# Centring x for the first layer norm with one fp32 product, without the rounded part and the remainder

## The chip, the cores and the metric

The kernel runs on one core of a Trainium2 chip. The metric is the device time of one execution in microseconds (us), the median of several runs. A measurement of this kernel repeats within about 0.1%.

## The reference, cut to what matters

Two Swin transformer blocks run on x of shape (16, 28, 28, 64), and a whitening over all tokens follows. Only the first layer norm of each block bears on the change:

```
def layer_norm(x, g, b):
    mu = jnp.mean(x, axis=-1, keepdims=True)
    var = jnp.var(x, axis=-1, keepdims=True)
    return (x - mu) * jax.lax.rsqrt(var + EPS) * g + b

def swin_block_fn(x, shift, mask, ...):
    y = layer_norm(x, ln1_g, ln1_b)
    ...                       # windows of 7x7 tokens, 8 heads, softmax attention
    x = x + out
    z = layer_norm(x, ln2_g, ln2_b)
    z = jax.nn.gelu(z @ fc1_w + fc1_b, approximate=False)
    return x + (z @ fc2_w + fc2_b)
```

## The kernel before, in words

The work is cut into 16 groups (`HALVES`) a block. A group is 392 tokens (`TOK`, eight windows of 49) of each of two images; the 64 channels of the two images share the 128 partitions, so x of a group is a tile of 128 x 392 in `XW`. Each block has an attention part, whose steps run over the groups, and an MLP part, whose steps run over the same groups. Each engine has its order of work written out by hand, and semaphores tie the engines together.

The norm of a group has these stages. TensorE multiplies x with the matrix `centre` (identity minus 1/64 within one image), which gives x minus its mean in the PSUM bank `bX` and counts up `xc_ready`. ScalarE squares it (`square`), TensorE averages the squares (`f_var`), ScalarE adds epsilon (`variance`, line 477), and VectorE computes the inverse root in eight instructions (lines 777 to 786) and the product with the centred x (line 789). That is `z_done`, which also frees `bX`. In the attention part this runs three groups ahead (`AHEAD = 3`).

There are two ways to form the centred x. `f_xc` multiplies `centre` and x as fp32. It serves the groups 0 to 3 of each block, and the MLP part has its own copy of it. `f_xc_split` serves the groups 4 to 15 of each block, in the steps 1 to 12. For it, ScalarE writes x rounded to the type fp32r into `xh` (`x_high`, line 485), GpSimd writes the remainder x minus `xh`, rounded too, into `xl` (`x_low`, line 402), and TensorE adds two products of fp32r operands in one accumulation, `centre_r` with `xh` and `centre_r` with `xl`.

An attention step of TensorE runs in this order: transposed scores of window group 0, the product of the probabilities with v for group 1 of the step before, v of the next step, scores of the next step for window group 0, **the centred x**, the output projection of the group two steps back (`proj`, four records `att,wph`), scores of the next step for window group 1 (its bias products are `bn,dup_r`; they wait for VectorE's row maxima, line 799), the averaged squares (`sq,conb`), k and q, transposed scores of group 1, and the next product with v. ScalarE rounds x behind the copies of k and q (lines 492 and 501) and ahead of the exponentials of window group 1 (line 518). GpSimd takes the remainder behind the two multiplications of the step, `attn` (line 409). SyncE issues all transfers of the steps; none of them carries `xh` or `xl`.

All matmuls of the steps have line 1008, so they are told apart by their operands: `xh,centre_r` and `xl,centre_r` are the two products of the split form, `XW,conb` is an fp32 product with `centre`, and `sq,conb` is one with the matrix of averages. An fp32 matmul stands in the trace as two records with a weight load each, and an fp32r one as one record.

Of the kernel before, what the change touches and what calls it, by code (L numbers as in the profile page):

```python
# [16 lines left out]
HALVES = 2 * PAIRS  # L17
# [40 lines left out]
def build(nc, x, par, gamma, beta, con, out):  # L58

    ctx = ExitStack()  # L60
    with ctx:
        def sb(name, shape, dt=F32):
            return ctx.enter_context(nc.sbuf_tensor(name, shape, dt))

        def sem(name):
            return ctx.enter_context(nc.semaphore(name))
# [54 lines left out]

        epsc = sb("epsc", [128, 1])

        xh = sb("xh", [128, TOK], F32R)
        xl = sb("xl", [128, TOK], F32R)
        sq = sb("sq", [128, TOK])
        lv = [sb(f"lv{i}", [128, TOK]) for i in range(2)]
        ly = sb("ly", [128, TOK])
# [67 lines left out]
        xc_ready, sq_done, var_ready, var_used, ln_link = (  # L196
            sem("xc_ready"), sem("sq_done"), sem("var_ready"), sem("var_used"), sem("ln_link"))

        xh_done, xl_done = sem("xh_done"), sem("xl_done")
        q_ready, k_ready, v_ready, s_ready, mxt_ready, st_ready, av_ready, proj_ready = (  # L200
            sem("q_ready"), sem("k_ready"), sem("v_ready"), sem("s_ready"), sem("mxt_ready"), sem("st_ready"),
            sem("av_ready"), sem("proj_ready"))
# [28 lines left out]
            return XW[blk][:, bass.ds(g * TOK, TOK)]  # L231

        AHEAD = 3
        NSPLIT = HALVES - AHEAD - 1
        NPREP = 6
        NCON, NPAR = 2, 3
        WSTEP = {n: i + 1 for i, n in enumerate(
# [135 lines left out]
        @block.gpsimd  # L373
        def _(pool):
            for k in range(2):
                for name in ("wq", "wk"):
                    nc.gpsimd.memset(P[k][name][:, :], 0.0)
                for name in ("f1", "f2"):
                    nc.gpsimd.memset(P[k][name][:, :, :], 0.0)
            nc.gpsimd.memset(wcol[:, EXPO:EXPO + 1], -0.5).then_inc(s_zero, 1)  # L380
            for i in range(2):
                nc.gpsimd.memset(vbd[i][:, :, :], 0.0)
            nc.gpsimd.memset(ones1[:, :], 1.0)
            for i in range(2):
                nc.gpsimd.memset(tsb[i][:, :, :, CH:CH + 1], 1.0)
            nc.gpsimd.memset(epsc[:, :], LN_EPS).then_inc(s_zero, 1)
            nc.gpsimd.memset(kexp[:, :, :], 0.0).then_inc(s_zero_x, 1)
            for i in range(2):
                nc.gpsimd.memset(qexp[i][:, :, :], 0.0).then_inc(s_zero_x, 1)
            pool.wait_ge(s_zero, 2)  # L390
            pool.wait_ge(s_zero_x, 3)

            for i in range(2):
                for w in range(2):
                    last = nc.gpsimd.memset(vbd[i][64 * w:64 * w + NTOK, :, 16 * w + HD:16 * w + HD + 1], 1.0)
            last.then_inc(s_zero, 1)

            def x_low(blk, g):

                pool.wait_ge(xh_done, NSPLIT * blk + g)  # L400
                pool.wait_ge(xc_ready, HALVES * blk + g + AHEAD)
                nc.gpsimd.tensor_tensor(xl[:, :], xcols(blk, g + AHEAD), xh[:, :].bitcast(F32), ALU.subtract)\
                    .then_inc(xl_done, 1)

            def attn(g, part):

                pool.wait_ge(rec_in[part], 16 * (g + 1))
                pool.wait_ge(proj_ready, g)
                nc.gpsimd.tensor_tensor(  # L409
                    att[:, 4 * part:4 * part + 4, :], osb[part][:, :].rearrange("p (a n) -> p a n", a=4),  # L410
                    rec[part][:, :].rearrange("p (a n) -> p a n", a=4), ALU.mult).then_inc(att_done, 1)

            def step(base, g):
                if g:
                    attn(base + g - 1, 0)
                    attn(base + g - 1, 1)
                if g + 1 + AHEAD < HALVES:
                    x_low(base // HALVES, g + 1)

            pool.wait_ge(s_con, 16 * NCON)  # L420
            for blk in range(2):
                base = HALVES * blk
                for g in range(HALVES):
                    step(base, g)
                attn(base + HALVES - 1, 0)
                attn(base + HALVES - 1, 1)

                if blk:
                    pool.wait_ge(w_dve, WSTEP["shift"])
                for it in range(0, PAIRS):  # L430
                    if blk == 0:
                        pool.wait_ge(mres_done, (it + 1) * 2)
                    pool_relay(pool, blk, it)

            pool.wait_ge(w_dve, WSTEP["trace"])
            nc.gpsimd.tensor_tensor(wcol[:, RSQ:RSQ + 1], wcol[:, TRACE:TRACE + 1], wcol[:, EXPO:EXPO + 1], ALU.pow)\
                .then_inc(w_pool, 1)
# [3 lines left out]
        def _(act):  # L441
# [34 lines left out]
                    act.wait_ge(z_done, g - 1)  # L476
                nc.scalar.activation(lv[buf][:, :], bB[:, 0:TOK], ACT.Identity, bias=epsc[:, 0:1]).then_inc(var_used, 1)  # L477

            def x_high(blk, g):

                if blk:
                    act.wait_ge(relay_done, (g + AHEAD) // 2 + 1)
                act.wait_ge(xc_ready, HALVES * blk + g + AHEAD)
                act.wait_ge(xl_done, NSPLIT * blk + g - 1)
                nc.scalar.activation(xh[:, :], xcols(blk, g + AHEAD), ACT.Copy).then_inc(xh_done, 1)

            def evac_k(p, g1, early=False):

                act.wait_ge(k_ready, g1 + 1)
# [37 lines left out]
            def step(p, base, g, u, first, ahead, tail=None, pair=0):  # L527

                G = base + g
                f = first and base == 0  # L530
                expo(G, 0, f)
                if first:
                    variance(G + 2, u)
                else:
                    o_copy(G - 1, 1, base == 0 and g == 1)
                if tail:
                    tail[0]()
                if ahead > 0:
                    evac_v(G + 1, 1 - u, f)
                if ahead > 2:  # L540
                    square(G + 3)
                    variance(G + 3, 1 - u)
                if ahead > 1:
                    evac_k(p, G + 2, f)
                    evac_q(p, G + 2, u, (G + 1) // 2 + 1)
                if g + 1 + AHEAD < HALVES:
                    x_high(base // HALVES, g + 1)
                expo(G, 1, f)
                if tail:
                    tail[1]()  # L550
                o_copy(G, 0, f)
# [454 lines left out]
        def _(pe):  # L1006
# [4 lines left out]

                mm(bX[:, 0:TOK], centre[:, :], xcols(blk, g - HALVES * blk)).then_inc(xc_ready, 1)

            def f_xc_split(blk, g):

                pe.wait_ge(xl_done, NSPLIT * blk + g)
                mm(bX[:, 0:TOK], centre_r[:, :], xh[:, :], True, False)
                mm(bX[:, 0:TOK], centre_r[:, :], xl[:, :], False, True).then_inc(xc_ready, 1)

            def f_var(g):  # L1020

                pe.wait_ge(sq_done, g + 1)
# [84 lines left out]
            def step(p, blk, g, u, ahead, tail=None, pair=0):  # L1107

                G = HALVES * blk + g
                first = g == 0  # L1110
                nb = 1 - u
                scores_t(p, blk, u, G, 0, u, pair, None if first else lambda i: (exp_done, 4 * G - 1 + i))
                if first:
                    pe.wait_ge(q_done, G + 2)
                    f_var(G + 2)
                else:
                    pv(G - 1, 1, nb)
                if ahead > 0:
                    pe.wait_ge(k_done, G + 2)
                    f_v(p, nb)  # L1120
                    scores(p, blk, nb, G + 1, 0, lambda i: (exp_done, 4 * G + 1 + i))
                if ahead > 2:
                    pe.wait_ge(z_done, G + 3)
                    if first:
                        if blk:
                            pe.wait_ge(relay_done, AHEAD // 2 + 1)
                        f_xc(blk, G + AHEAD)
                    else:
                        f_xc_split(blk, g)
                if g > 1:  # L1130
                    pe.wait_ge(v_done, 2 * G + 4 if ahead > 0 else 2 * G + 2)
                    proj(p, G - 2)
                if ahead > 0:
                    scores(p, blk, nb, G + 1, 1, lambda i: (max_done, 4 * G + 5 + i))
                if tail:
                    tail[0]()
                if ahead > 2:
                    if first:
                        pe.wait_ge(var_used, G + 3)
                    f_var(G + 3)  # L1140
                if ahead > 1:
                    if g > 1:
                        pe.wait_ge(res_done, G - 1)
                    else:
                        pe.wait_ge(v_done, 2 * G + 4)
                    f_qk(p, G + 2, u, (var_used, G + 4) if ahead > 2 else (rx_done, G + 1))
                scores_t(p, blk, u, G, 1, u, pair,
                         (lambda i: (max_done, 4 * G + 7 + i)) if ahead > 0 else lambda i: (exp_done, 4 * G + 1 + i))
                if tail:
                    tail[1]()  # L1150
                if ahead > 0:
                    if ahead > 1:
                        pe.wait_ge(q_done, G + 3)
                    maxt(G + 1)
                pv(G, 0, u, first and blk == 0)
# [345 lines left out]
```

## Time and profile before

| what | value |
|---|---|
| time, median of 3 runs | 910.91 us (910.0 to 911.21) |
| the profiled execution | 913.9 us, of which the span of the trace is 912.1 us |
| mean granted TensorE clock | 0.941 of full speed |
| busy: TensorE, its weight loads, VectorE, ScalarE, GpSimd | 820.0, 565.1, 588.5, 378.6, 218.2 us |
| attention stretches with the 24 split products | 96 to 290 us and 494 to 697 us of the span |

The profile is one execution. The names PE, PEld, DVE, ACT, POOL and SP stand for TensorE's matmuls, its weight loads, VectorE, ScalarE, GpSimd and SyncE. "Idle before" is idle time of the engine ahead of the instruction, and behind the arrow is what ended it; "issue" is idle time in which the engine waited for nothing that the profile shows. Matmuls are pipelined and overlap, so what one costs the stream is the distance between its start and the start of the next, not its own duration. In a view by windows the columns are the window and its length, then the busy time (and instructions) of PE, PEld, DVE, ACT and POOL, the granted clock as a share of full speed, the busy share of the DMA engines and their GB/s. [...]

### The profile page before, as it was taken

Reading aid. Unit: us, or ns where it says so; the run is one execution under the profiler, and the core shown is the slowest. Engines: PE = TensorE matmul, PEld = TensorE weight load, DVE = VectorE, ACT = ScalarE, POOL = GpSimd, SP = SyncE. Lnnn points to the kernel's source line nnn. Section 1 sums busy time; section 2 is a strip of 40 time slices with the busy share of each in tenths; the row PEclk is TensorE's granted clock in tenths of the full one; section 3 lists DMA queues with packets and bytes.
Section 4 is the critical chain, followed back from the end, with each engine's and each line's share of the span. In section 5 each row is a group of like instructions: output and inputs, shape, how many; then the busy total and the mean of one; then the engine's idle time right before and its main releaser. Section 6 shows DMA issues by size and latency. Waiting matters only on the chain.

```text
span 912.1 us, 35605 instructions
## 1 busy us (share of the span) xinstructions
PE 820.0 (90%) x15686; PEld 565.1 (62%) x15686; DVE 588.5 (65%) x1047; ACT 378.6 (42%) x676; POOL 218.2 (24%) x507
## 2 busy tenths in 40 slices
PE   3777899998999889999859999999999989999968
PEld 2645677676776655555436676776667645555648
DVE  2636887676778448888655666767666378887033
ACT  1513445354443344455423444544444345454400
POOL 4000122122120103435400211212211026565100
PEclk9768999999999889999977999999999989999959
DMA  9100121121111110000001111112112110000004
GB/s 225 19 29 24 46 62 56 44 63 57 51 63 48 59 33 10 1 1 0 19 19 32 59 51 52 60 50 66 50 45 68 34 40 0 1 1 0 2 0 142
DMA packets 47662, 38.34 MB, mean 42 GB/s; under 512 B 28564, under 2 KB 46996, under 8 KB 47508
## 3 DMA queue, kind: packets, MB, share of 16 engines
q1 hardware_dynamic: 46496, 33.96, 12.8%
q8 instruction: 124, 2.03, 0.9%
q10 hardware_dynamic: 1012, 2.10, 0.7%
q14 instruction: 30, 0.25, 0.1%
HBM read 18.37 MB, written 4.01 MB: 25 GB/s over the span
## 4 chain that ended last, share of the span: by engine, by line
PE 44%; DVE 3%; issue 2%; DMA 1%; ACT 0%; SPq 0%; POOL 0%; DVEq 0%; ACTq 0%
PE psum L1008 43%; DVE nmax L799 1%; PE psum L1370 1%; DMA dens<-rpk 1%; DMA rec<-dens 0%; DVE kexp L980 0%; ACT lv L477 0%; DVE kexp L982 0%; DVE lt L779 0%; DVE ly L786 0%; DVE lt L780 0%; DVE lt L785 0%; POOL att L409 0%; DVE ly L777 0%; DVE z L789 0%
## 5 line engine op out<-in xcount | busy, mean ns | idle before, releaser
L409 POOL TENSOR_TENSOR att<-osb,rec 128x392 f32<-128x392 f32 x64 | 72.0, 1125 | 425.0 <-DMA rec<-dens 406.0
L799 DVE TENSOR_REDUCE nmax<-psum 113x16 f32<-113x784 f32 x128 | 118.5, 968 | 71.7 <-PE psum L1008 71.7
L518 ACT ACTIVATE pt<-psum 113x784 f32<-113x784 f32 x128 | 98.6, 822 | 122.2 <-PE psum L1008 122.2
L610 ACT ACTIVATE hid<-psum,vecb 128x392 f32<-128x392 f32 x128 | 75.1, 587 | 96.9 <-PE psum L1008 92.4
L1008 PE MATMUL psum<-bt,dup_r 113*113 113x392 f32 x256 | 102.6, 401 | 2.3 <-DVE nmax L799 2.1
L1008 PE MATMUL psum<-z,f 128*128 128x392 f32 x256 | 97.5, 504 | 0.1
L1008 PE MATMUL psum<-hid,f 128*128 128x392 f32 x256 | 89.9, 493 | 0.0
L1008 PE MATMUL psum<-rx,sel_r 128*113 128x392 f32 x256 | 88.6, 346 | 0.0
L1008 PE MATMUL psum<-kexp,qsb 32*49 32x98 f32 x4096 | 73.7, 262 | 10.4 <-issue 9.8
L825 DVE RECIPROCAL rpk<-dpk 64x49 f32<-64x49 f32 x64 | 28.9, 452 | 76.1 <-DMA dpk<-osb 76.0
L1008 PEld LDWEIGHTS psum<-kexp,qsb 32*49 32x49 f32 x4096 | 57.0, 123 | 30.2 <-issue 29.2
L1008 PEld LDWEIGHTS psum<-z,f 128*128 128x128 f32 x256 | 49.3, 194 | 38.5 <-ACT hid L610 3.0
L1008 PEld LDWEIGHTS psum<-hid,f 128*128 128x128 f32 x256 | 48.5, 190 | 35.4
L367 POOL TENSOR_TENSOR XW<-XW,wcol 128x49 f32<-128x49 f32 (+5 forms) x200 | 59.1, 332 | 42.3 <-DVE XW L890 31.2
L1008 PE MATMUL psum<-qexp,ksb 32*49 32x98 f32 x4096 | 68.4, 252 | 0.5 <-issue 0.5
L1008 PE MATMUL psum<-pt,vbd 113*32 113x49 f32 x4096 | 60.8, 210 | 7.0 <-ACT osb L525 5.6
L1008 PEld LDWEIGHTS psum<-qexp,ksb 32*49 32x49 f32 x4096 | 54.3, 118 | 19.0 <-issue 18.6
L1008 PE MATMUL psum<-sq,conb 128*128 128x392 f32 x128 | 61.4, 564 | 5.1 <-ACT sq L592 2.8
L349 POOL COPY XW<-XW 128x64 f32<-128x64 f32 (+2 forms) x192 | 47.5, 304 | 57.0 <-DVE XW L890 57.0
L1008 PEld LDWEIGHTS psum<-pt,vbd 113*32 113x32 f32 x4096 | 51.6, 111 | 14.0 <-issue 8.6
L777 DVE TENSOR_SCALAR ly<-lv 128x392 int32<-128x392 int32 x64 | 23.8, 372 | 56.0 <-ACT lv L477 26.7
L477 ACT ACTIVATE lv<-psum,epsc 128x392 f32<-128x392 f32 x32 | 18.8, 588 | 92.8 <-PE psum L1008 91.5
(154 smaller groups left out, 1321.7 us busy)
## 6 DMA issues: line engine op xcount, KB each, us to landing
rec<-dens SPq DMA_DIRECT2D x64, 196.0 KB
kexp<-ksb SPq DMA_DIRECT2D x128, 49.0 KB
qexp<-qsb SPq DMA_DIRECT2D x128, 49.0 KB
XW<-x_dram SPq DMA_DIRECT2D x14, 196.0 KB, 4.7
out_dram<-XW SPq DMA_DIRECT2D x14, 196.0 KB, 2.4
dpk<-osb SPq DMA_DIRECT2D x64, 12.2 KB
dens<-rpk SPq DMA_DIRECT2D x64, 12.2 KB, 2.6
pt<-w_dram ACTq DMA_DIRECT2D x2, 384.0 KB, 7.4
```

The source lines that it names most:

```text
L349: last = nc.gpsimd.tensor_copy(dst[:, i, jo:jo + jn, ro:ro + rn, co:co + cn], src[:, si, ji:ji + jn, ri:ri + rn, ci:ci + cn])
L367: last = nc.gpsimd.tensor_tensor(dst[:, y0:y0 + rn, q0:q0 + cn], src[:, i, j, r0:r0 + rn, c0:c0 + cn], wcol[:, SHIFTC:SHIFTC + 1].rearrang ...
L409: nc.gpsimd.tensor_tensor(att[:, 4 * part:4 * part + 4, :], osb[part][:, :].rearrange("p (a n) -> p a n", a=4), rec[part][:, :].rearrange( ...
L477: nc.scalar.activation(lv[buf][:, :], bB[:, 0:TOK], ACT.Identity, bias=epsc[:, 0:1]).then_inc(var_used, 1)
L518: nc.scalar.activation(pt[grp][:, b:b + 2, :], SC[0:KROWS, b:b + 2, 0:BANK], ACT.Exp)\
L610: nc.scalar.activation(hid[c], mF1[c % 2][:, 0:TOK], ACT.Gelu, bias=p["vec"][:, FB + c:FB + c + 1]).then_inc(gelu_done, 1)
L777: ln(nc.vector.tensor_scalar(ly[:, :].bitcast(I32), v[:, :].bitcast(I32), -0.5, MAGIC, ALU.mult, ALU.add))
L799: nc.vector.tensor_reduce(nmax[:, GWIN * grp:GWIN * grp + GWIN, :].rearrange("p w (g a) -> p a w g", g=2)[:, b:b + 2], SC[0:KROWS, b:b + 2 ...
L825: nc.vector.reciprocal(rpk[part][:, :], dpk[part][:, :]).then_inc(rec_done, 1)
L1008: return nc.tensor.matmul(o, a, b, start=start, stop=stop, **k)
L1370: last = nc.tensor.transpose(PS[4 + part][0:TILE, t * 128:(t + 1) * 128], XR[:, c0:c0 + TILE], ident[:, :])
```

## The change

The steps 1 to 12 of each block form the centred x with `f_xc`, as the other groups do. The tiles `xh` and `xl`, the instructions that write them and their two semaphores go. In the second block TensorE now waits itself for `relay_done`, the count of image pairs that GpSimd has moved into the shifted order. The place of the product in TensorE's order stays, and so does its wait for `z_done`.

```diff
--- before.py
+++ after.py
@@ -121,8 +121,6 @@
 
         epsc = sb("epsc", [128, 1])
 
-        xh = sb("xh", [128, TOK], F32R)
-        xl = sb("xl", [128, TOK], F32R)
         sq = sb("sq", [128, TOK])
         lv = [sb(f"lv{i}", [128, TOK]) for i in range(2)]
         ly = sb("ly", [128, TOK])
@@ -196,7 +194,6 @@
         xc_ready, sq_done, var_ready, var_used, ln_link = (
             sem("xc_ready"), sem("sq_done"), sem("var_ready"), sem("var_used"), sem("ln_link"))
 
-        xh_done, xl_done = sem("xh_done"), sem("xl_done")
         q_ready, k_ready, v_ready, s_ready, mxt_ready, st_ready, av_ready, proj_ready = (
             sem("q_ready"), sem("k_ready"), sem("v_ready"), sem("s_ready"), sem("mxt_ready"), sem("st_ready"),
             sem("av_ready"), sem("proj_ready"))
@@ -231,7 +228,6 @@
             return XW[blk][:, bass.ds(g * TOK, TOK)]
 
         AHEAD = 3
-        NSPLIT = HALVES - AHEAD - 1
         NPREP = 6
         NCON, NPAR = 2, 3
         WSTEP = {n: i + 1 for i, n in enumerate(
@@ -395,13 +391,6 @@
                     last = nc.gpsimd.memset(vbd[i][64 * w:64 * w + NTOK, :, 16 * w + HD:16 * w + HD + 1], 1.0)
             last.then_inc(s_zero, 1)
 
-            def x_low(blk, g):
-
-                pool.wait_ge(xh_done, NSPLIT * blk + g)
-                pool.wait_ge(xc_ready, HALVES * blk + g + AHEAD)
-                nc.gpsimd.tensor_tensor(xl[:, :], xcols(blk, g + AHEAD), xh[:, :].bitcast(F32), ALU.subtract)\
-                    .then_inc(xl_done, 1)
-
             def attn(g, part):
 
                 pool.wait_ge(rec_in[part], 16 * (g + 1))
@@ -414,8 +403,6 @@
                 if g:
                     attn(base + g - 1, 0)
                     attn(base + g - 1, 1)
-                if g + 1 + AHEAD < HALVES:
-                    x_low(base // HALVES, g + 1)
 
             pool.wait_ge(s_con, 16 * NCON)
             for blk in range(2):
@@ -475,14 +462,6 @@
                 if not first:
                     act.wait_ge(z_done, g - 1)
                 nc.scalar.activation(lv[buf][:, :], bB[:, 0:TOK], ACT.Identity, bias=epsc[:, 0:1]).then_inc(var_used, 1)
-
-            def x_high(blk, g):
-
-                if blk:
-                    act.wait_ge(relay_done, (g + AHEAD) // 2 + 1)
-                act.wait_ge(xc_ready, HALVES * blk + g + AHEAD)
-                act.wait_ge(xl_done, NSPLIT * blk + g - 1)
-                nc.scalar.activation(xh[:, :], xcols(blk, g + AHEAD), ACT.Copy).then_inc(xh_done, 1)
 
             def evac_k(p, g1, early=False):
 
@@ -543,8 +522,6 @@
                 if ahead > 1:
                     evac_k(p, G + 2, f)
                     evac_q(p, G + 2, u, (G + 1) // 2 + 1)
-                if g + 1 + AHEAD < HALVES:
-                    x_high(base // HALVES, g + 1)
                 expo(G, 1, f)
                 if tail:
                     tail[1]()
@@ -1011,12 +988,6 @@
 
                 mm(bX[:, 0:TOK], centre[:, :], xcols(blk, g - HALVES * blk)).then_inc(xc_ready, 1)
 
-            def f_xc_split(blk, g):
-
-                pe.wait_ge(xl_done, NSPLIT * blk + g)
-                mm(bX[:, 0:TOK], centre_r[:, :], xh[:, :], True, False)
-                mm(bX[:, 0:TOK], centre_r[:, :], xl[:, :], False, True).then_inc(xc_ready, 1)
-
             def f_var(g):
 
                 pe.wait_ge(sq_done, g + 1)
@@ -1121,12 +1092,9 @@
                     scores(p, blk, nb, G + 1, 0, lambda i: (exp_done, 4 * G + 1 + i))
                 if ahead > 2:
                     pe.wait_ge(z_done, G + 3)
-                    if first:
-                        if blk:
-                            pe.wait_ge(relay_done, AHEAD // 2 + 1)
-                        f_xc(blk, G + AHEAD)
-                    else:
-                        f_xc_split(blk, g)
+                    if blk:
+                        pe.wait_ge(relay_done, (g + AHEAD) // 2 + 1)
+                    f_xc(blk, G + AHEAD)
                 if g > 1:
                     pe.wait_ge(v_done, 2 * G + 4 if ahead > 0 else 2 * G + 2)
                     proj(p, G - 2)
```

## Rows read from the trace of the kernel before

**Rows 1.** The page: busy time of each engine, then the chain that ended last:
```profile
PE 820.0 (90%) x15686; PEld 565.1 (62%) x15686; DVE 588.5 (65%) x1047; ACT 378.6 (42%) x676; POOL 218.2 (24%) x507
...
PE 44%; DVE 3%; issue 2%; DMA 1%; ACT 0%; SPq 0%; POOL 0%; DVEq 0%; ACTq 0%
```

**Rows 2.** Busy time by engine in the two attention stretches, with the clock:
```profile
96.00:290.00 194.00, 185.69 (x5383) 136.22 (x5366) 145.79 (x235) 90.50 (x153) 41.09 (x35) 1.00 0.19 56
494.00:697.00 203.00, 192.09 (x5457) 141.01 (x5456) 139.03 (x228) 92.19 (x156) 39.09 (x35) 0.97 0.18 54
```

**Rows 3.** Who TensorE waited for: total us, times, longest; the first stretch, then the second:
```profile
PE psum L1008 <- issue: 6.6, 9, 1.5
...
PE psum L1008 <- DVE nmax L799: 1.4, 3, 0.5
...
PE psum L1008 <- issue: 9.9, 13, 1.7
...
PE psum L1008 <- DVE nmax L799: 1.0, 2, 0.5
```

**Rows 4.** Order of time, start and us, TensorE in one step:
```profile
160.75 0.45 PE L1008 MATMUL psum<-xh,centre_r 128*128 128x392 f32 x1
...
161.22 1.51 PE L1008 MATMUL psum<-att,wph 128*128 128x392 f32 x4
...
162.66 0.64 PE L1008 MATMUL psum<-bn,dup_r 49*113 49x392 f32 x4
...
164.18 0.93 PE L1008 MATMUL psum<-sq,conb 128*128 128x392 f32 x2
...
164.95 0.82 PE L1008 MATMUL psum<-z,wk 128*128 128x392 f32 x2
```

**Rows 5.** All instructions on the tile xh (min, median, max ns; first and last start):
```profile
L485 ACT ACTIVATE xh<-XW x24: 519/522/524, 85.8 to 671.8; 128x392 fp32r<-128x392 f32 x24
...
L402 POOL TENSOR_TENSOR xl<-XW,xh x24: 1012/1184/1437, 86.4 to 674.0; 128x392 fp32r<-128x392 f32 x24
```

**Rows 6.** Order of time of TensorE at the low clock, then a window there:
```profile
499.12 1.68 PE L1008 MATMUL psum<-sq,conb 128*128 128x392 f32 x2
...
500.59 1.51 PE L1008 MATMUL psum<-z,wk 128*128 128x392 f32 x2
...
647.84 0.69 PE L1008 MATMUL psum<-xh,centre_r 128*128 128x392 f32 x1
...
648.66 2.41 PE L1008 MATMUL psum<-att,wph 128*128 128x392 f32 x4
...
647.10:650.50 3.40, 3.40 (x42) 2.31 (x33) 2.22 (x3) 0.72 (x2) 0.00 (x0) 0.50 0.04 8
```

**Rows 7.** Order of time, TensorE in two steps with a wait behind the product:
```profile
96.16 0.45 PE L1008 MATMUL psum<-xh,centre_r 128*128 128x392 f32 x1
...
97.30 0.43 PE L1008 MATMUL psum<-bn,dup_r 49*113 49x392 f32 x2 [0.51 <-DVE nmax L799]
...
180.49 0.43 PE L1008 MATMUL psum<-bn,dup_r 49*113 49x392 f32 x2 [0.42 <-DVE nmax L799]
```

**Rows 8.** Order of time, TensorE just before the clock fell:
```profile
645.76 0.32 PE L1008 MATMUL psum<-wv,z 64*49 64x64 f32 x4 [1.74 <-issue]
```

**Rows 9.** Order of time, ScalarE behind the rounded copy in one step:
```profile
169.25 1.54 ACT L518 ACTIVATE pt<-psum 113x784 f32<-113x784 f32 x2 [1.49 <-PE psum L1008]
```

**Rows 10.** Order of time, GpSimd and VectorE in one step, then its next product:
```profile
205.58 1.35 POOL L402 TENSOR_TENSOR xl<-XW,xh 128x392 fp32r<-128x392 f32 x1
...
206.08 1.28 DVE L786 SCALAR_TENSOR_TENSOR ly<-lt,ly 128x392 f32<-128x392 f32 x1
...
207.39 0.57 DVE L789 TENSOR_TENSOR z<-psum,ly 128x392 f32<-128x392 f32 x1
...
211.63 0.45 PE L1008 MATMUL psum<-xh,centre_r 128*128 128x392 f32 x1
```

**Rows 11.** Who GpSimd waited for in the first stretch:
```profile
POOL att L409 <- DMA rec<-dens: 159.0, 24, 13.5
```

## The prediction

> **What bounds the kernel now.** I read the page first. TensorE is busy in 90% of the span, and the chain that ended last lies on it for 44%; the other engines have 3% at most [rows 1]. (The rest of the chain is not put down to an engine, so I do not rest on that share alone.) Then I cut out the two stretches in which the split products run. In the first TensorE is busy for 185.69 of 194 us, in the second for 192.09 of 203, while VectorE has 146 and 139 us and ScalarE 90 and 92 [rows 2]. The waits say what the rest is: in both stretches together 2.4 us end with the row maxima of VectorE, and 16.5 us in 22 gaps are "issue", in which TensorE waited for nothing that the profile shows [rows 3]. It waits nowhere for `xl`, for `xh` or for the norm's last product. So in these stretches each thing that TensorE does is paid for in time, and what the other three engines do is covered. That is how every part of the change is priced below.
>
> **What the change takes away.** On ScalarE 24 rounded copies of 0.522 us go, 12.5 us in sum [rows 5]. Each stands right ahead of the exponentials of window group 1, and in the step shown ScalarE is idle for 1.49 us behind the copy until TensorE has those scores [rows 9]. Without the copy it waits for 2.0 us instead of 1.5. Cost 0. If that cover were gone, the gain would be 0.5 us a step.
>
> On GpSimd 24 remainders of 1.18 us go, 28 us in sum [rows 5]. Behind them in its queue are the two multiplications by the softmax's reciprocals, and these wait for their transfers for 159 us in the first stretch alone, 6.6 us at a time [rows 11]. Without the remainder GpSimd is idle earlier. Cost 0.
>
> The remainder also slows VectorE. With the one at 205.58 running, the norm's instruction at 206.08 takes 1.28 us where the product at 207.39, of the same size, takes 0.57 [rows 10]. One to two instructions are slowed by a remainder, so the change gives VectorE 0.7 to 1.4 us in such a step. But the centred x scaled there is complete at 207.96, and the next thing that needs it, the product at 211.63, starts 3.7 us later, and not because of it [rows 10]. Cost 0 again: the margin grows.
>
> [...]
>
> No transfer is added or removed. The waits for `xh_done` and `xl_done` go. The new wait of TensorE for `relay_done` costs nothing: ScalarE waited for the same counts a step earlier before it rounded x, and all these copies are done in the MLP part.
>
> **What it adds on TensorE.** The split form takes from the start of `xh,centre_r` at 160.75 to the start of the projection at 161.22, which is 0.47 us of the stream. An fp32 product with 392 columns and the same kind of place (behind the small score products) is `sq,conb`: from 164.18 to 164.95, 0.77 us [rows 4]. So one product costs 0.30 us more. The other bound is the projection, two fp32 products in a row, from 161.22 to 162.66: 0.72 us each, which makes 0.25 us more. I take 0.30, since in both cases the product follows the small ones. At the low clock the same two distances are 1.47 us (499.12 to 500.59) and 0.82 us (647.84 to 648.66), so 0.65 us more [rows 6].
>
> [...]
>
> **What of it is covered.** Behind the product and the projection come the bias products that wait for VectorE. In the first step of a block there is no projection, and TensorE has a wait of 0.51 us for the row maxima, until 97.30 [rows 7]. The new product would be done at 96.16 + 0.77 = 96.93, so nothing is lost; this is so in both blocks. In the step of 177.75 there is such a wait of 0.42 us, until 180.49 [rows 7], which covers it too. The maxima waited for there are of scores that TensorE finished before the product, so the new product doesn't delay them. That is three of 24. Of the 21 others, two run at the low clock: the one shown at 647.84 [rows 6] and one like it in an interval of the same length in the same stretch, whose mean clock is 0.97 [rows 2].
>
> **Sum.** 19 x 0.30 + 2 x 0.65 = 5.7 + 1.3 = 7.0 us. The profiled execution took 913.9 us (912.1 of it the span), so its like would take 920.9. The median of the runs was 910.91, 3 us below the profiled one, and the added work is the same in both: 917.9 us. With 0.25 and 0.50 us a product it is 5.8 us. With nothing covered it is 7.9 us.
>
> **The rivals.**
> *Gaps take it up.* The 22 issue gaps are not tied to data. If TensorE is held there until something arrives at a set time, a product that ran longer just before is partly free. At 0.30 us for each of 22 gaps that is 6.6 us, and the time would be within 0.2% of before, 911.3 us. Against it: in the steps that I looked at the gap lies ahead of the product in the small products, and the next is a step or two away. Half of this is likelier than all of it: 914.6 us.
> *Gaps go away.* This is the rival on the other side. The first of two waits ahead of the product goes in the first block, so TensorE's instructions are one fewer a step, and each gap meets another place of the step. It decides from 8.8 us on, more than half of the 16.5 us [rows 3]: with 10 us of gaps gone the time is 907.9 us. The trace shows no reason for gaps to shrink rather than to grow.
> *VectorE was a hidden bound.* The freed 0.7 to 1.4 us a step would give back at most all that TensorE waits for VectorE, 2.4 us [rows 3]: 917.9 - 2.4 = 915.5 us. It cannot turn the sign.
> *The clock.* An idle time of 1.74 us ended at 645.76 [rows 8], and from 647.10 the granted clock was 0.50 for 3.4 us [rows 6], which costs 1.7 us where TensorE is the bound. Longer or other gaps could bring two more such falls or take away the two that the second stretch has behind its gaps: two more make 921.3 us. A denser TensorE speaks against more of them.
>
> **How the numbers follow.** A measurement of this kernel can tell about 0.2% (1.8 us) from no change. Chances: the sum as worked out, 916 to 919.5 us, 0.60; the gaps or unseen waits take up part, 912.8 to 916 us, 0.13; VectorE gives back its 2.4 us, 0.05; more falls of the clock or longer gaps, 919.5 to 923 us, 0.12; all taken up, 0.05; gaps gone, faster, 0.05. Slower is thus 0.90, the same 0.05, faster 0.05. The range goes from the middle of the partly covered case to the middle of the clock's: 914 to 921 us, which leaves out 0.18.
>
> **What would show each step.** In the changed profile 24 more products `XW,conb` stand in the steps, each with two records, and the projection starts 0.77 us behind the first of them at full clock; if it is 0.47 us, the price is wrong. The two attention stretches become longer by some 3.0 us (ten products) and 4.0 us (nine, and two at the low clock), and the rest of the span stays. GpSimd's busy time falls by 28 us, ScalarE's by 12.5, VectorE's by 10 to 20, and TensorE's waits for them stay near 2.4 us. If the time does not rise, the issue gaps have shrunk from 16.5 us by as much, or the clock's low intervals in the stretches have gone. The prediction is wrong if the steps contain a wait that I read as TensorE's own work, above all the distances inside the stream of small products, or if the gaps move by more than the sum.

## The result, and the profile after

The changed kernel has a median of 917.9 us over 20 runs (911.2 to 927.09), the kernel before 911.65 us over 20 runs beside it (908.14 to 915.0). The ratio is 1.0053 with a 95% interval of 1.0033 to 1.0073, so 3.0 to 6.7 us slower, most likely 4.8. (The ratio leaves out two slow runs, 926.0 and 927.09 us, which the median contains.) A second series of the same kernel is among the experiments: 1.0072, 1.0035 to 1.0109. The profiled execution took 917.54 us with a span of 915.8 us, 3.7 us more than the span before.

The page of the changed kernel, busy time and the chain that ended last:
```profile
PE 821.6 (90%) x15686; PEld 560.3 (61%) x15686; DVE 580.1 (63%) x1047; ACT 369.0 (40%) x652; POOL 187.4 (20%) x483
...
PE 43%; DVE 3%; issue 2%; DMA 1%; ACT 0%; SPq 0%; POOL 0%; DVEq 0%; ACTq 0%
```
Beside [rows 1], GpSimd is busy for 30.8 us less, ScalarE for 9.6 and VectorE for 8.4 (none of its instructions went: its 1047 instructions became shorter). The span became longer all the same. TensorE's matmul records are as many as before, since two fp32r records became two fp32 ones.

The two attention stretches by windows, each moved to about the same points of the work as in [rows 2]:
```profile
96.00:293.00 197.00, 189.95 (x5400) 136.66 (x5392) 141.40 (x234) 86.84 (x144) 25.79 (x24) 1.00 0.18 56
498.00:700.00 202.00, 190.91 (x5457) 137.51 (x5456) 135.21 (x227) 87.47 (x144) 26.56 (x24) 1.00 0.18 54
```
The granted clock of the second stretch is 1.00, where it was 0.97. The three low-clock intervals in it (at 497, 531 and 647 us) are not in this execution. Measured between the same two points of the work, from the first product of a stretch to the projection of step 12, the first stretch became 3.2 us longer (179.7 to 183.0), as forecast (3.0). The second became 1.2 us shorter (187.4 to 186.2) where 4.0 more was forecast: its first step alone went from 20.4 to 17.0 us, about what the 6.8 us at half the clock from 497 us cost in it before (an estimate: half of them, 3.4 us). How far one execution can be off shows in the kernel of "The relief alone" below. It has the TensorE stream of the kernel before, and its second stretch took 180.1 us.

What TensorE waited for in these windows, the first stretch and then the second:
```profile
PE psum L985 <- issue: 6.0, 11, 1.0
PE psum L985 <- DVE nmax L776: 0.7, 2, 0.4
...
PE psum L985 <- issue: 10.6, 13, 1.6
PE psum L985 <- DVE nmax L776: 0.7, 2, 0.4
```
The issue gaps are 16.6 us in 24 pieces, against 16.5 in 22 [rows 3]. The waits for the row maxima went from 2.4 to 1.4 us: part of them now lies under the longer product.

One step of TensorE in order of time, the rows that answer to [rows 4]:
```profile
162.32 0.93 PE L985 MATMUL psum<-XW,conb 128*128 128x392 f32 x2
163.08 1.50 PE L985 MATMUL psum<-att,wph 128*128 128x392 f32 x4
164.51 0.62 PE L985 MATMUL psum<-bn,dup_r 49*113 49x392 f32 x4
```
The new product takes from 162.32 to 163.08, 0.76 us, in this and in the other 21 steps that have a projection. The split form took 0.47 (0.466 in the middle of its 20 steps at full clock). The projection behind it takes 1.43 us, as before.

The first step of the first block, which answers to the first two of [rows 7]:
```profile
96.39 0.93 PE L985 MATMUL psum<-XW,conb 128*128 128x392 f32 x2
97.54 0.44 PE L985 MATMUL psum<-bn,dup_r 49*113 49x392 f32 x2 [0.23 <-DVE nmax L776]
```
The bias products start 1.15 us behind the start of the product, and before it was 1.14 us. The wait fell from 0.51 to 0.23 us: this product costs nothing.

ScalarE and VectorE in order of time, in two other steps:
```profile
171.01 1.54 ACT L497 ACTIVATE pt<-psum 113x784 f32<-113x784 f32 x2 [1.83 <-PE psum L985]
```
```profile
208.01 0.57 DVE L766 TENSOR_TENSOR z<-psum,ly 128x392 f32<-128x392 f32 x1
```
ScalarE now waits 1.83 us for the scores, where it waited 1.49 [rows 9]. VectorE has the norm's product done at 208.58, and TensorE's next centring product starts at 213.12, 4.5 us later, where the margin was 3.7 [rows 10]. What the change freed has become idle time.

### The profile page after: what moved, and what is told of

Read it like the earlier page. It is cut to its first block and busy times, and to the rows that moved or that the text cites. A ratio compares the mean times of both kernels' runs of the same rounds, so it can differ in the third digit from the quotient of the medians.

```text
span 915.8 us, 35497 instructions
## 1 busy us (share of the span) xinstructions
PE 821.6 (90%) x15686; PEld 560.3 (61%) x15686; DVE 580.1 (63%) x1047; ACT 369.0 (40%) x652; POOL 187.4 (20%) x483
## 5 line engine op out<-in xcount | busy, mean ns | idle before, releaser
L398 POOL TENSOR_TENSOR att<-osb,rec 128x392 f32<-128x392 f32 x64 | 69.8, 1090 | 566.7 <-DMA rec<-dens 458.9
L985 PE MATMUL psum<-XW,conb 128*128 128x392 f32 x128 | 61.2, 562 | 12.3 <-DVE z L766 11.1
L985 PEld LDWEIGHTS psum<-pt,vbd 113*32 113x32 f32 x4096 | 52.3, 111 | 16.6 <-issue 11.4
```

What stands on the lines that cost most here:

```text
L398: nc.gpsimd.tensor_tensor(att[:, 4 * part:4 * part + 4, :], osb[part][:, :].rearrange("p (a n) -> p a n", a=4), rec[part][:, :].rearrange( ...
L985: return nc.tensor.matmul(o, a, b, start=start, stop=stop, **k)
```

## Taking the stretch apart

Every attention step has the same sequence of matmul records, so the steps of one execution can be laid on each other. For 20 steps (ten of each block, from the projection of step 2 to that of step 12) the distance between two neighbouring starts was compared with the median of the same place over the 20 steps. What lies above it was put down to one of three causes: it stands where TensorE's count of instructions, taken by 256, comes round to one fixed remainder (a crossing; see the last section), it lies in a low-clock interval, or neither. The rest is the stream without disturbance. Each line below is from one profiled execution, worked out from its trace, and in us:

```
                         stream     crossings  low clock  other  total
kernel before            307.2      16.9       2.8        3.0    329.7
changed kernel           312.6      19.2       0          3.4    335.1
changed, second series   312.9      17.9       1.4        2.4    334.6
```

The stream of 20 steps grew by 5.4 to 5.8 us, 0.27 to 0.29 us a product. Where exactly the stream ends and a disturbance begins is a matter of the split, by up to 1 us: the plain sums of the medians are 307.3, 313.6 and 312.6 us, a growth of 5.3 to 6.3. Group by group the medians changed at the product alone, from 0.46 to 0.76 us; every other group of a step kept its length within 0.02 us. The crossings cost 1.0 to 2.3 us more, although the change moves them by twelve records at most, and the low clock gave back 1.4 to 2.8. So the price of the product is plain in one step, and the time of one execution is not: all disturbances together (22 us) are about four times the size of the change.

## The experiments

Eleven kernels ran, each beside the kernel before on the same chip, in three groups. The ratios are to the kernel before of the same group, whose medians were 908.4, 908.6 and 907.7 us. Beside the first result it was 911.65. With single executions from 901 to 915 us, the repetition within 0.1% said at the start was too good: the intervals below are 0.2 to 0.4% to either side.

### The changed kernel again

> The changed kernel itself, unaltered, beside the two kernels that vary it. Theory: 24 products at 0.29 us more, of which TensorE's stream pays for 21 or more: ratio 1.004 to 1.008. Rival (its first result owed much to low-clock intervals or gaps of that one series): ratio under 1.003.

Measured: 1.0072 (1.0035 to 1.0109), median 913.99 against 908.61 us. The slowing is there in a second series. Its profile is the third line of the table above.

### The relief alone

```diff
-                if g + 1 + AHEAD < HALVES:
-                    x_low(base // HALVES, g + 1)
+                if g == 0 and base == 0:
+                    x_low(0, 1)
...
-                pe.wait_ge(xl_done, NSPLIT * blk + g)
+                pe.wait_ge(xl_done, 1)
```
(and `x_high` in the same way)

> Left out: the rounded copy and the remainder are formed once, for the first of the 24 products, and the other 23 multiply those old tiles. TensorE's stream is that of the kernel before; 23 copies of 0.52 us on ScalarE and 23 remainders of 1.2 us on GpSimd are gone. Theory (only TensorE's stream counts here): ratio to before 1.000, within 0.998 to 1.002. Rival (VectorE, slowed by the remainders, or ScalarE was a hidden bound): up to 2.4 us less, ratio 0.997, or lower.

Measured: 1.0016 (0.9988 to 1.0043). Its stream of 20 steps is 307.0 us against 307.2. The page shows the relief in full:
```profile
PE 812.5 (90%) x15686; PEld 559.9 (62%) x15686; DVE 574.4 (64%) x1047; ACT 368.5 (41%) x653; POOL 190.2 (21%) x484
```
GpSimd is at 190.2 instead of 218.2 us and VectorE at 574.4 instead of 588.5, and the time did not fall. The rival that VectorE was a hidden bound has fallen: a gain of 2.4 us would have been 0.9974, outside the interval.

### The product alone

```diff
-                mm(bX[:, 0:TOK], centre_r[:, :], xh[:, :], True, False)
-                mm(bX[:, 0:TOK], centre_r[:, :], xl[:, :], False, True).then_inc(xc_ready, 1)
+                mm(bX[:, 0:TOK], centre[:, :], xcols(blk, g + AHEAD)).then_inc(xc_ready, 1)
```

> The other half of the change: copies and remainders go on as before and TensorE still waits for the remainder, but it forms the centred x in one fp32 product from x. Theory: the whole cost of the change, 0.29 us for each of some 21 products that nothing covers, 6 us, ratio 1.007, and equal to the changed kernel within the noise. Rival (the freed engines give something back in the changed kernel): ratio above that of the changed kernel, 1.009 or more.

Measured: 1.0030 (1.0007 to 1.0053), 0.6 to 4.8 us. It is slower than before, but the expected 1.007 lies outside the interval. The trace shows the product at its price:
```profile
175.46 0.93 PE L1008 MATMUL psum<-XW,conb 128*128 128x392 f32 x2
176.22 1.50 PE L1008 MATMUL psum<-att,wph 128*128 128x392 f32 x4
```
The distance is 0.76 us and the stream of 20 steps is 313.0 us, 5.9 more than before and within half a us of the changed kernel. So the stream carries the whole price with the copies in place, and the rival that they gave something back is not borne out: this kernel is not slower than the changed one. The interval overlaps with those of both series of the changed kernel. Why the series lies lower than its stream says is not settled; the expectation was too narrow.

### The product twice

```diff
+                    if g:
+                        mm(bX[:, 0:TOK], centre[:, :], xcols(blk, g + AHEAD))
                     f_xc(blk, G + AHEAD)
```

> The changed kernel with the fp32 product written twice in the 24 places, the first result overwritten. Theory: each further product costs its two records of 0.33 us, 24 x 0.66 = 15.8 us above the changed kernel less what three to five row-maximum waits cover, so 13 to 16 us, ratio to before 1.021 to 1.024. Rival (idle time behind the product takes up a good part of what is added there): under 8 us above the changed kernel, ratio under 1.015.

Measured: 1.0255 (1.0214 to 1.0297), median 929.64 against 908.44 us. Less the 1.0072 of the changed kernel that makes 16.6 us, and less the 1.0053 of its first series 18.3, where 13 to 16 was expected; the changed kernel did not run in this group, and the interval is 3.8 us to either side. The stream is 326.3 us, 13.7 above the changed kernel in 20 steps, 0.69 us for a further product. Time added at this place is paid for in full; nothing behind it takes up more than the three waits.

### The rounded part alone

```diff
-                mm(bX[:, 0:TOK], centre_r[:, :], xh[:, :], True, False)
-                mm(bX[:, 0:TOK], centre_r[:, :], xl[:, :], False, True).then_inc(xc_ready, 1)
+                mm(bX[:, 0:TOK], centre_r[:, :], xh[:, :]).then_inc(xc_ready, 1)
```

> Left out: the second fp32r product, so the remainder is formed but not added. Theory: TensorE has one record of 0.18 us less in 24 places, 4.3 us, ratio 0.995 to 0.996. Rival (the stream is held by something else in most steps): ratio 0.999 to 1.001.

Measured: 1.0029 (1.0003 to 1.0055). The theory's 4.3 us less did not come. TensorE in order of time in one of its steps:
```profile
195.75 0.45 PE L1008 MATMUL psum<-xh,centre_r 128*128 128x392 f32 x1
196.04 1.50 PE L1008 MATMUL psum<-att,wph 128*128 128x392 f32 x4
197.47 0.73 PE L1008 MATMUL psum<-bn,dup_r 49*113 49x392 f32 x4
```
The product takes 0.29 us, 0.18 less, as expected. But the four bias products behind the projection take 0.73 to 0.81 us where they took 0.61 to 0.64: they now come before the row maxima are ready. In all 20 steps the second pair of them starts 0.05 to 0.06 us behind the end of a row maximum of VectorE; in the kernel before most of these pairs start 0.17 to 0.21 us behind it, and that difference was the whole margin. Over 20 steps the stream is only 1.3 us shorter (305.9), not 3.6. So the kernel before stood at the edge: what is added to TensorE here is paid for, and what is taken away is mostly refilled by the wait for VectorE. Even 1.3 us less should not give a ratio above 1. That remainder is of the size of the crossings (18.4 us in its profile against 16.9), and it is open.

### The same number of instructions, and all crossings moved

In the first block the change leaves one wait where there were two ahead of the product, and TensorE's records are 31,726 instead of 31,738, twelve fewer. The first of these two kernels puts a wait back, the second moves every crossing of the kernel before by 64 instructions:

```diff
                     pe.wait_ge(z_done, G + 3)
+                    if g and not blk:
+                        pe.wait_ge(s_round, 1)
```
```diff
+            pe.wait_ge(s_tpcp, 2 * PAIRS)
+            for _ in range(16):
+                mm(PS[4][:, 0:1], ident[:, :], ident[:, 0:1])
             pe.wait_ge(s_round, 1)
```

> The changed kernel with one further wait on an old semaphore value ahead of the product in the steps of the first block, so that TensorE's instructions are as many in each step as in the kernel before. Theory of the gaps (each issue gap stands where TensorE crosses into its next 256 instructions): the records of the kernel before and of this one cross at the same places of each step, the gaps stand at the same places, and the time is that of the changed kernel within 2 us. Rival (the drift by one instruction a step moved gaps that matter): over 2 us off the changed kernel, either way.

Measured: 1.0061 (1.0029 to 1.0092), median 913.44 against the 913.99 us of the changed kernel in the same group. These series don't show that the twelve instructions matter, and the stream of its profile (312.4 us as the sum of the medians) is that of the changed kernel.

> The kernel before with 16 one-column fp32 matmuls (64 instructions) into an unused bank while TensorE waits for its constants at the start, where they cost under 2 us or nothing. Theory of the gaps: all gaps of the attention steps move back by 64 instructions of the stream, still one place in 256, and their sum changes, so the time may move by up to 5 us either way from the kernel before. Rival (the gaps belong to places in the work, such as the score products, and not to a count): they stay at the same operands and places.

Measured: 1.0045 (1.0015 to 1.0076). TensorE in order of time, first the kernel before, then this one, in the same step:
```profile
142.62 0.63 PE L1008 MATMUL psum<-bn,dup_r 49*113 49x392 f32 x4
143.18 0.54 PE L1008 MATMUL psum<-kexp,qsb 32*49 32x98 f32 x20
144.60 0.82 PE L1008 MATMUL psum<-kexp,qsb 32*49 32x98 f32 x44 [0.88 <-issue]
```
```profile
144.81 0.92 PE L1008 MATMUL psum<-wv,z 64*49 64x64 f32 x25
147.10 0.42 PE L1008 MATMUL psum<-wv,z 64*49 64x64 f32 x7 [1.37 <-issue]
147.45 0.61 PE L1008 MATMUL psum<-bn,dup_r 49*113 49x392 f32 x4
```
The gap stood behind the 20th of the score products and now stands behind the 25th of v's, which is 20 + 4 + 7 = 31 matmuls with as many weight loads earlier, 62 instructions of the 64 that were put in (the records around a gap can't be ordered more exactly). The theory of the gaps holds, and the rival that they belong to a place in the work has fallen. The stream is 306.9 us, that of the kernel before, and yet the series is 0.15 to 0.76% slower, 1.4 to 6.9 us. The trace shows where: the 16 matmuls of one column were expected to cost under 2 us, and did not. The kernel before at this place, then this one:
```profile
43.04 2.95 PE L1008 MATMUL psum<-rec,conb 49*113 49x392 f32 x4 [1.40 <-DVE rec L734]
47.78 1.65 PE L1008 MATMUL psum<-z,wk 128*128 128x392 f32 x2 [1.78 <-DVE tabt L734]
```
```profile
42.17 2.95 PE L1008 MATMUL psum<-rec,conb 49*113 49x392 f32 x4 [1.41 <-DVE rec L734]
45.06 6.98 PE L1008 MATMUL psum<-conb 128*128 128x1 f32 x32
51.90 1.66 PE L1008 MATMUL psum<-z,wk 128*128 128x392 f32 x2
```
They took 6.98 us at a granted clock of 0.50, and the product of `z` and `wk` starts 9.73 us behind the row above it where it was 4.74: 5.0 us later. That is as much as the series lost, so it leaves nothing that the new places of the crossings would have to explain, and says little of what they are worth.

### Squares in rounded form: what TensorE's stream is worth

```diff
-        sq = sb("sq", [128, TOK])
+        avg_r = sb("avg_r", [128, 128], F32R)
+        sq = sb("sq", [128, TOK], F32R)
...
-                mm(bB[:, 0:TOK], avg64[:, :], sq[:, :]).then_inc(var_ready, 1)
+                mm(bB[:, 0:TOK], avg_r[:, :], sq[:, :]).then_inc(var_ready, 1)
```
(the second norm in the same way; VectorE fills `avg_r` at the start)

> The kernel before, with the squares written by ScalarE as fp32r and averaged in one fp32r product, in both norms of both blocks, 64 places. Each place loses one of two records: 0.48 us in the attention steps (0.77 to 0.29) and 0.48 us in the MLP. Theory (TensorE's stream pays for everything in the steps): 64 x 0.48 = 31 us less where nothing covers it, 24 to 31 us, ratio 0.966 to 0.974. Rival (what is taken out of the stream is refilled by waits for the row maxima or the norm, as the single rounded product showed): under 12 us, ratio above 0.987.

Measured: 0.9748 (0.9709 to 0.9788), median 886.71 against 908.61 us, 19 to 26 us less. That is the largest effect of all, though below the 24 to 31 us of the theory for the better part of its interval.
```profile
177.49 0.45 PE L1011 MATMUL psum<-sq,avg_r 128*128 128x392 f32 x1
177.78 0.82 PE L1011 MATMUL psum<-z,wk 128*128 128x392 f32 x2
```
The averaged squares take 0.29 us where they took 0.77 [rows 4], and the stream of 20 steps is 297.0 us, 10.2 less: the full price of 0.5 us a step. In the same 20 steps the crossings went from 16.9 to 21.5 us and other waits from 3.0 to 5.9. This is where 7.5 of the 10.2 us went in that execution, and the 20 steps became only 2.4 us shorter (329.7 to 327.3). In the MLP the gain arrives whole: the distance over 23 groups (12 of the first block, 11 of the second) fell by 11.1 us, 0.48 us a group. So in these two profiles the MLP, and not the attention steps, has the sure part of the gain.

### On top of the rounded squares

The change itself on that kernel, then the rounded part alone without the remainder, then the same with the remainder formed but not added:

> The change made on the kernel with rounded squares. Theory: its price is the same there, 0.29 us in 21 to 24 places, 6 to 7 us above the kernel with rounded squares: ratio to before 0.980 to 0.983. Rival (with 0.48 us less in the step a chain outside TensorE holds it, and the product hides): ratio 0.973 to 0.977.

Measured: 0.9775 (0.9738 to 0.9813). By the middle values that is 2.5 us above the kernel with rounded squares, and the two intervals overlap. Between the theory's 6 and the rival's 0 this series doesn't decide. The distance of 0.76 us is there in its steps, and by the plain sums of the medians its stream is 304.7 us against 297.1 for the rounded squares alone. But the 20 steps as a whole are not longer in that execution (323.6 against 327.3 us), since crossings and low clock cost less in it.

> Left out: the remainder and its product; the centred x comes from the rounded x alone, in one fp32r product, on the kernel with rounded squares. This is the candidate for the best version. Theory: 0.18 us less in 24 places, of which the row maxima take up half or more, 1 to 4 us below the kernel with rounded squares: ratio to before 0.970 to 0.974. Rival (nothing gained, as the one product alone showed): ratio 0.974 to 0.978.

Measured: 0.9743 (0.9707 to 0.9779), median 885.37 us. This run has the lowest median.

> Left out: the product with the remainder, which is still formed; the squares are rounded. Theory (GpSimd's and VectorE's time is free): the same as without the remainder, within 0.3%, ratio 0.970 to 0.974. Rival (the remainders, which slow VectorE, now cost time because the row maxima end a wait in most steps): 2 us or more above the kernel that has no remainders.

Measured: 0.9749 (0.9716 to 0.9783), median 886.34 us. The series don't tell it from the kernel without the remainders; they could not show less than some 3 us. The traces have a sign against "free": with rounded squares TensorE waits for VectorE's `rx` (the spread row maxima), 2.6 us in 9 waits between 111 and 274 and between 498 and 663 us with the remainders and 1.7 us in 6 without them, which it did nowhere in these stretches of the kernel before, and by the plain sums of the medians the stream is 301.0 us here against 297.2 without the remainders. Whether the remainders cost time here is open. Neither kernel is told apart from the kernel that keeps the remainder's product (0.9748). So of what beats both kernels, the rounded squares are the whole gain, and they can be had with the split form kept.

## Why the prediction was right

**The number: a hit to the tenth, which is luck.** Forecast and median are both 917.9 us. But the kernel before was at 911.65 us beside it and not at 910.91, and the single executions of the changed kernel spread over 16 us. The ratio says 3.0 to 6.7 us more, so the forecast rise of 7.0 us lies just above the first series, and within the second (3.2 to 9.9 us). Nor do the series alone prove the price: the four series with one fp32 product have 1.0030 to 1.0072, and the single rounded product, with a shorter stream, has 1.0029. What shows it is the stream, and the product twice.

**TensorE is the bound, and what the others do is covered: shown.** With the relief alone the stream is 307.0 against 307.2 us and the ratio 1.0016. With the product alone the stream is that of the changed kernel.

**0.30 us more for a product: right.** It is 0.763 - 0.466 = 0.30 us in the middle of the 20 full-clock steps that can be compared one by one, and 0.27 to 0.29 us as a mean over the stream (0.32 at most by the other split). The bound taken from the projection (0.25) was the worse one, since the product does follow the small ones. 0.76 is 1.6 times 0.47, and the records, from start to start, show how each is made up: the first of the split form takes 0.28 us and the second 0.18, the first of the fp32 product 0.43 and the second 0.33 (medians of 22 steps, before and after; in the kernel with the product twice the second, third and fourth take 0.33 each). The single rounded product, a first record alone, takes 0.28 to 0.29. So in both forms the first record takes 0.10 us more than one that follows it: 0.47 is 0.1 + 2 x 0.18, and 0.76 is 0.1 + 2 x 0.33.

**Three products covered: the first steps right, the third by chance.** The first step lost nothing (1.15 us against 1.14). The wait in the step of 177.75 was one of that execution and is not there in the changed one.

**Two products at the low clock, 1.3 us: this term was mis-sized, by its count.** No low-clock interval met a product in the profiled execution after, and at full clock the two cost 0.6. The price of 0.65 us was right: in the second series' profile one product fell into such an interval (at 562.72 us) and took 1.47 us, where the split form took 0.82. The sum with the measured price, 22 x 0.30, is 6.6 us in place of 7.0. Against the first series it is still at the upper end (3.0 to 6.7 us), and within the second. The low-clock intervals are not fixed places of the kernel (none in the second stretch of the profile after, one from 561.9 us in that of the second series), and should have stood in the range and not in the sum.

**The relief.** 24 copies of 0.522 us were to take 12.5 us from ScalarE's busy time, and it fell by 9.6: each copy had overlapped the instruction ahead of it by 0.10 us, which is 2.4 of the 2.9 us between them. GpSimd fell by 30.8 us (28 predicted), VectorE by 8.4 us, less than predicted (10 to 20): fewer or shorter slowdowns than one to two a remainder, each sized by the 1.28 us of the norm's instruction beside a remainder [rows 10] (the median of its 64 is 0.57 us). None of it bears on the time.

**The rivals.** VectorE as a hidden bound has fallen. That gaps take the product up has fallen as well, as the product twice shows. That gaps go away or grow stays true as a source of scatter: the crossings differ by up to 2.3 us between two executions here. That they would fall by the 8.8 us or more which this rival needed was seen in none of the profiles. More falls of the clock did not come in the two attention stretches; there were none after and one in the second series, against three before.

## What to carry to other kernels

Where one engine is busy for 95% of a stretch, price a change by the distances between starts in that engine's own stream, at the same kind of place, and count what the other engines gain as nothing until a wait names them. Splitting an fp32 operand into two rounded ones pays here because the helpers' time is free: the split form is 0.3 us cheaper in each of the 22 places where nothing covers it, although it adds 40 us of work on two idle engines. Before paying for the remainder, try whether one rounded product is enough somewhere in the kernel: the average of the squares was such a place. It took 0.48 us out of TensorE's stream in each of 64 places, 31 us, of which 19 to 26 us (2.1 to 2.9%) arrived in the time.

## What was not expected

The issue gaps of TensorE are tied to its count of instructions. Count all of its records (matmuls, weight loads and waits) in order of start. In the 20 steps of each of the thirteen profiles, 10 to 15 gaps are over half a us and without a named releaser, 158 in all, and every one of them stands at the same remainder of that count by 256, 193 or 194. (Outside the 20 steps one at 195 was seen, the one before the product at 514.92 of the kernel before.) One of the changed kernel:
```profile
529.67 0.43 PE L985 MATMUL psum<-bn,dup_r 49*113 49x392 f32 x1
531.39 0.51 PE L985 MATMUL psum<-bn,dup_r 49*113 49x392 f32 x3 [1.30 <-issue]
```
And a queue of instructions on the page, which by its count is TensorE's:
```profile
q8 instruction: 124, 2.03, 1.0%
```
Its 124 packets have 16 KB each, and TensorE has 31,726 records, 124 times 256 but for 18. Just ahead of the gap shown a packet ran from 528.71 to 529.96; TensorE was idle from 530.09 and went on at 531.39, 1.4 us behind the packet's end. In all 158 gaps this distance is 1.2 to 1.6 us. Count and distance together say that TensorE waits there for its own instructions. Most crossings cost little: of some 71 in 20 steps only 16 to 24 cost over 0.3 us, depending on the profile, but all together they cost 17 to 19 us in the table above, over 5% of the time of these steps. The small products use up 256 instructions in 1.7 us where they are densest (the kernel before, from start to start). A step has 914 instructions (913 in the first block of the changed kernel), 3.57 times 256, so a crossing comes back every second step, each time some 18 matmuls earlier in it.
